# Whole levels of the sigmoid: from VectorE and ScalarE by turns to GpSimd alone, in a two-layer cross-attention and feed-forward kernel

## What is computed

```python
def act_qdq(x):
    scale = jnp.maximum(jnp.max(jnp.abs(x)) / qmax, 1e-12)
    return jnp.clip(jnp.round(x / scale), -qmax - 1.0, qmax) * scale
def fixed_qdq_u16(x):
    scale = 1.0 / 65536.0
    return jnp.clip(jnp.round(x / scale), 0.0, 65535.0) * scale
x = act_qdq(x)
up = act_qdq(x @ lpbq_dequant(w_up).T)
gate = act_qdq(x @ lpbq_dequant(w_gate).T)
sig = fixed_qdq_u16(jax.nn.sigmoid(gate))
gate = act_qdq(gate * sig)
o = act_qdq(gate * up)
return o @ lpbq_dequant(w_down).T
```

## Time and profile before

| | us |
|---|---|
| median of three runs (lowest, highest) | 1559.03 (1558.42, 1559.81) |
| the profiled execution's own time | 1561.33 |
| its span in the profile | 1559.6 |
| busy in the span: PE, DVE, ACT, POOL | 1280.5, 1042.2, 809.1, 522.7 |

### The profile page before, as it was taken

The page is one execution under the profiler, slowest core; times in us unless marked ns, Lnnn a source line. Parts: engine busy times, 40 slices in busy tenths (PEclk is TensorE's granted clock), DMA queues, the critical chain, the costliest instruction groups (busy, mean ns, idle before and its releaser), DMA issues. The chain is left out here.

```text
span 1559.6 us, 29136 instructions
## 1 busy us (share of the span) xinstructions
PE 1280.5 (82%) x8823; PEld 967.2 (62%) x8824; DVE 1042.2 (67%) x1908; ACT 809.1 (52%) x1173; POOL 522.7 (34%) x430
## 2 busy tenths in 40 slices
PE   5859899967987574989699999552399999999996
PEld 3426667753433364856366766552399989899895
DVE  4947997765589695548488888555156566656653
ACT  0535455654499596525477777551144343444431
POOL 1026677600000000010476766077223323333233
PEclk9979999988999556968899999655699999999998
DMA  5010000000033674000122122545222222222220
GB/s 207 1 65 1 1 0 0 0 1 0 0 122 161 212 237 164 9 1 0 58 69 83 65 70 92 217 167 186 84 46 49 45 47 44 45 42 51 47 42 9
DMA packets 63213, 106.87 MB, mean 69 GB/s; under 512 B 9712, under 2 KB 50768, under 8 KB 62000
## 3 DMA queue, kind: packets, MB, share of 16 engines
q1 hardware_dynamic: 48848, 89.17, 17.2%
q0 software_dynamic: 14304, 16.93, 6.1%
HBM read 67.89 MB, written 40.01 MB: 69 GB/s over the span
## 5 line engine op out<-in xcount | busy, mean ns | idle before, releaser
L2125 POOL DMA_INDIRECT out<-ex_yo,ex_mt x78 | 132.1, 1693 | 320.0 <-DVE ex_yo L2100 172.8
L2002 PE MATMUL ex_ps_h<-ex_xT_hi,a_arena 128*128 128x256 f16 x1248 | 212.8, 274 | 0.0
L2044 ACT ACTIVATE ex_hT<-ex_ps_h,e_b1T,e_unscale 128x256 f32<-128x256 f32 x312 | 150.9, 564 | 115.4 <-PE ex_ps_h L2002 115.4
L708 PE MATMUL at_ps_s<-a_arena,at_xnT_hi 128*128 (+1 forms) x512 | 162.8, 401 | 34.0 <-issue 26.7
L730 PE MATMUL at_ps_y<-c_VW,at_pT_hi 128*128 (+1 forms) x1024 | 171.1, 273 | 1.3 <-DVE main_x_res L857 1.3
L2002 PE MATMUL ex_ps_h<-ex_xT_lo,a_arena 128*128 128x256 f16 x624 | 171.1, 274 | 0.0
L2015 PE MATMUL ex_ps_y<-a_arena,ex_hT_lo 128*128 x624 | 170.1, 273 | 0.0
L2015 PE MATMUL ex_ps_y<-e_w_lo,ex_hT_hi 128*128 x624 | 170.1, 273 | 0.0
L2015 PE MATMUL ex_ps_y<-a_arena,ex_hT_hi 128*128 x624 | 170.1, 273 | 0.0
L976 POOL TENSOR_TENSOR at_sc<-at_sc,at_ri 128x960 f32<-128x960 f32 (+1 forms) x96 | 133.4, 1403 | 83.5 <-DVE at_ri L852 83.2
L1217 PE MATMUL gm_bank<-f_xq,f_wide 128*128 (+1 forms) x576 | 129.1, 384 | 20.8 <-ACT gm_stg L1255 16.2
(11 more groups left out here) (321 smaller groups left out, 2847.8 us busy)
## 6 DMA issues: line engine op xcount, KB each, us to landing
at_half<-in_L_ffn_W SPq DMA_DIRECT2D x32, 512.0 KB, 4.3
up_scratch<-gm_stg SPq DMA_DIRECT2D x16, 768.0 KB, 3.2
gm_stg<-up_scratch SPq DMA_DIRECT2D x16, 768.0 KB, 4.3
ex_row<-xs SPq DMA_DIRECT2D x39, 260.0 KB, 2.7
rt_stage<-in_L_ffn_W SPq DMA_DIRECT2D x16, 512.0 KB, 5.3
main_x_res<-in_x SPq DMA_DIRECT2D x8, 512.0 KB, 11.9
out<-main_x_res SPq DMA_DIRECT2D x4, 1024.0 KB, 12.3
xs<-rt_pad SPq DMA_DIRECT2D x18, 130.0 KB, 2.3
```

What stands on the lines that cost most here:

```text
L708: last = nc.tensor.matmul(ps_s[j][:, c * CH:(c + 1) * CH], a[:, d, :], b[:, d, bass.ds(off + c * CH, CH)], start=(n == 0), stop=(n == 3 * ...
L2002: last = nc.tensor.matmul(ps_h[:, n, :], a[:, bass.ds(e * WN + d * HID + n * P, P)], b[:, d, :], start=(m == 0), stop=(m == 3 * DT - 1))
L2044: last = nc.scalar.activation(hT[:, n, :], ps_h[:, n, :], ACT.Relu, bias=b1T[:, bass.ds(e * HT + n, 1)], scale=unscale[:, 0, bass.ds(e, 1)])
L2125: nc.gpsimd.indirect_dma_start(out=acc[:, :], out_offset=bass.IndirectOffsetOnAxis(ap=mt[j][:, q, 1:2].bitcast(U32), axis=0), in_=yo[j][:, ...
```

## The change

POOL makes the levels of all sixteen units; the halves of DVE and ACT and the semaphore `sqa_r` are gone. Product(u) waits for POOL's count.

```diff
@@ block.scalar
-                def sig_levels(u):
-                    act.wait_ge(sig_r, u + 1)
-                    nc.scalar.activation(sq[u % 2][:, :], unit(u), ACT.Copy, scale=65536.0).then_inc(sqa_r, 1)
@@
                 for u in range(NU):
                     up_out(u)
                     sigmoid(u)
-                    if u % 2:
-                        sig_levels(u)
                     if u + 1 < NU:
                         levels(u + 1)
@@ block.vector
-                def sig_levels(u):
-                    dve.wait_ge(sig_r, u + 1)
-                    nc.vector.tensor_scalar(sq[u % 2][:, :], unit(u), 65536.0, 65535.0, ALU.mult, ALU.min).then_inc(sq_r, 1)
                 def product(u):
-                    dve.wait_ge((sq_r, sqa_r)[u % 2], u // 2 + 1)
+                    dve.wait_ge(sq_r, u + 1)
                     nc.vector.tensor_tensor(unit(u), gq[u % 2][:, :], sq[u % 2][:, :], ALU.mult).then_inc(pr_r, 1)
@@
                 for u in range(NU):
                     up_max(u)
-                    if u % 2 == 0:
-                        sig_levels(u)
                     if u:
                         prod_max(u - 1)
                     product(u)
@@ block.gpsimd
                 for i in range(2):
                     nc.gpsimd.tensor_copy(ctxe[0:C1, i, :], ctxT[0:C1, 1, :]).then_inc(low_set, 1)
+                for u in range(NU):
+                    pool.wait_ge(sig_r, u + 1)
+                    need(pool, pr_r, u - 1)
+                    nc.gpsimd.tensor_scalar(sq[u % 2][:, :], unit(u), 65536.0, 65535.0, ALU.mult, ALU.min).then_inc(sq_r, 1)
                 pool.wait_ge(gred, 2)
                 nc.gpsimd.partition_all_reduce(allr[:, 1:3], red[:, 1:3], P, RMAX).then_inc(gall, 1)
```

More of the change, by code:

```diff
@@ L1201, in gated_mlp @@
             u_st = [z.sem(f"u_st{h}") for h in range(2)]
-            sqa_r = z.sem("sqa_r")
             gq_r, sig_r, sq_r, pr_r = z.sem("gq_r"), z.sem("sig_r"), z.sem("sq_r"), z.sem("pr_r")
```

## The result

| | before | after |
|---|---|---|
| median of four runs, us | 1559.34 (1558.42 to 1559.81) | 1588.29 (1587.93 to 1601.68) |
| span of the profiled execution | 1559.6 | 1599.9 |
| first to last all-reduce of scope "gu" | 93.63 | 124.82 |

The kernel is slower by 28.95 us: the ratio is 1.0207, with a 95% interval of 1.0154 to 1.0261, so the slowdown is clear and whether it is over 2% is not. That is outside the predicted range and on the side of the slow rival.

The account below looks back on a forecast made before the run. DVE was taken to bound the stretch: 7.16 us gained in the run, 6.71 lost before product(0) and 2.65 at the end gave +2.2, so 1559.0 + 2.2 = 1561.2 us, range 1554.7 to 1564.6.

Parts of the forecast that it names:

- the slow rival: POOL's level instruction exceeds 3.2 us and sets the beat with the product; at X = 4.0 1577.1 us, 18 slower; chance 0.12.
- What bounds the stretch: From 433 to 523 us DVE bounds the stretch, busy 85.85 of 90 us; product to product takes 4.99.
- relief for ACT: Removing ACT's eight copies gains nothing: its 4.66 us a unit stay hidden under DVE's 4.99.
- the sum: 7.16 us gained in the product steps, 6.71 lost before product(0), 2.65 at the end: +2.2 us.
- X = 2.3: Price in us of each of POOL's sixteen level instructions, taken from POOL's copy of 256 columns scaled to 1536.
- X up to 3.2 is hidden: DVE's two maxima hide a POOL level instruction up to 3.2 us, keeping the beat 4.99; 2.3 leaves 0.9 to spare.
- The rival's price for a unit: When POOL's level instruction exceeds 3.2 us, a unit takes X + 1.76 instead of 4.99; chance 0.12.
- They take turns whole: POOL's instruction and DVE's two-input product wait for each other at SBUF, so POOL starts unit u+2 when product(u+1) ends.
- The two loads: POOL library loads before the first level instruction, 8.5 us, and before the last all-reduce, 7.5 us.
- traffic and price go together: POOL's library loads cost more beside DMA traffic: 5.89 us in the quiet case, 7.58 to 9.86 in the other three.
- POOL first at the start: POOL's second level instruction precedes product(0), which starts at 445.6 instead of 438.89; with traffic-laden loads, chance 0.42.
- what follows product(15): Last level ends at 519.5, a 7.5 us load follows; the all-reduce starts at 527.0 against 524.82, 2.2 us later.

Follow-up runs that it names:

- e5: Changed kernel with POOL's level instruction as a plain copy, without scaling and clamp: stretch between all-reduces 86.96 us, kernel 1552.24 us against 1558.12 before.
- e2: Kernel before plus seven forms of POOL's instruction in the first stretch, at 1536 and 768 columns: at 1536 the change's form took 5.42 us, copies 1.46.
- e7: Changed kernel with POOL's level instruction as a two-input addition of 128, taken off in the product, no clamp: stretch 94.44 us, products 4.99 apart.
- e8: Kernel before with POOL making units 2 to 13 by the addition of 128, no clamp: 1554.30 us against 1558.12, ratio 0.9974.
- e6: Changed kernel with one arithmetic step in POOL's level instruction, clamp left out: stretch 106.37 us, products 5.74 apart.
- e3: Changed kernel with product(u) replaced by a maximum over `sq`, a single SBUF input: stretch 107.05 us, level instructions 5.37 to 5.42.
- e1: Changed kernel run again unedited on another chip: 1607.18 us against 1574.96 for the kernel before, ratio 1.0215.
- e4: Kernel before plus one single-column tensor_scalar on POOL behind the last product: stretch 97.53 us against 93.63.

## Why the prediction was wrong

**What bounds the stretch: right.** DVE did, and relief for ACT is worth nothing. Taking the level instruction off DVE at no other price gained 6.67 us (e5) where the sum had 7.16 less 0.5.

**X = 2.3: the step that failed.** "The nearest is POOL's copy", I wrote, and took its time, with the two-input operation as the bound above, 2.85. Measured: 5.42 (after, e2), over twice that, and so far over the 3.2 that DVE hides that POOL and its turns with the product set the beat. No row of the trace before was of this form, and I took for granted that an instruction with one input is cheaper than one with two. Here it is not: 1.46 for the copy, 2.75 for two inputs (e7, e8), 4.09 and 5.42 for one input with one and two arithmetic steps (e2). My 2.85 for two inputs from 1024 columns was near; my 2.35 for the copy from 256 was not.

**X up to 3.2 is hidden, beyond it POOL sets the beat: right as far as it was tried.** At X = 2.75 it was 4.99 (e7), at 4.09 it was 5.74 (e6), at 5.42 it was 7.02; nothing between 2.75 and 4.09 was run. The rival's price for a unit, X + 1.76, was 0.11 to 0.16 too high; X + 1.6 to 1.65 fits. The 1.61 us from POOL's end to DVE's in the earlier trace rows had been the nearer number.

**They take turns whole: right for this loop, too strong as a rule.** 5.42 becomes 6.95 beside a two-input product and stays 5.37 beside a one-input reduction (e3). SBUF — State Buffer of the Trainium skill (the section on the two sides) has the rule, an exclusive lock of the port pair held for a whole instruction, against a VectorE operation with two SBUF inputs; by that rule, the traces agree that one of the two waits, and not always that it waits to the end: where POOL was first, DVE's product had its turn before POOL's one-step form had ended (e2, e6), and the one at 397.66 in e2 ran inside POOL's instruction.

**The two loads: right in kind, mis-sized.** The first is 6.82 us, not 8.5, the second 5.94, not 7.5. I had read "traffic and price go together" out of four rows. In the runs since, the elementwise library took 6.8 to 7.1 us ahead of the level instruction with a DMA share of 0.33 or 0.34 beside it, no more than the 6.9 of e2 with 0.00. The all-reduce's took 5.8 to 6.2 with any share from 0.00 to 0.45, and 6.55 with 0.71 (e7). But the library alone does not decide either. The same traces have the loads of the earlier trace rows again: ahead of line 144 7.2 to 8.1 us, ahead of the second attention's addition of line 989 9.4 to 10.7 wherever "issue" ended it, ahead of the router's all-reduce (line 1698 before) 7.4 to 8.0 with a share of 0.80 to 0.84. So a high share goes with a longer load of the all-reduce's library, one like that of this stretch does not, and what makes line 989's so long stays open. GPSIMD Engine Reference of the Trainium skill (section 2.1) has about 6 us; for the all-reduce's library at low shares that agrees, for the elementwise one in this stretch it is 0.8 to 1.1 us short, and for those of lines 144, 989 and 1698 1.2 us or more.

**POOL first at the start: wrong in this kernel.** Product(0) was issued 0.05 us before POOL's second instruction and went first, in both profiled executions (0.04 in e1); in e6 and e7 POOL's second was issued 0.04 and 0.01 us before the product and went first. So the one issued first had its turn first in all four; what makes POOL's second instruction late with two arithmetic steps (0.08 us behind the first, where e6 has none) was not tried.

Put into the same steps, the missing number gives nearly the whole result. With X = 5.42 my own formulas, on the axis of before, have product(0) at 441.0 + 2 x 5.42 = 451.84, fifteen steps of 7.18 to 559.54, and the all-reduce 7.5 later at 567.04: +42.2. Measured was +31.2. The 11.0 between them are POOL first (5.4), the beat of 7.02 (2.3), the first load (1.7) and what follows product(15), 5.91 instead of 7.5 (1.6).

The slow rival, "POOL's instruction is longer than the 3.2 us it may take", is what happened. It had 0.12, and its size was set at X = 4.0 and +18. The words for it, "two arithmetic steps", named a part of the cause: the second step is 1.33 of the 5.42, and with one step alone the 4.09 is over 3.2 as well. Its "converts to 16 bits" was no part of it (5.42 against 5.38). The argument against it, "even the two-input operation scales to 2.85", was the failed step once more.

## What to carry to other kernels

When work moves to an engine on which the trace shows no instruction of the same form, the price of another form is no bound: widen the range by a factor rather than by a microsecond, and ask from which price on the new engine sets the beat. Count what an elementwise instruction on GpSimd brings beside itself: a library load before it and one before the next all-reduce, which are free only where POOL is idle long enough on both sides (e4, e8), and a turn at the port beside every two-input VectorE operation, and beside a one-input tensor_scalar as in e2. Keep the first and last units of such a loop on their old engines, and choose the form by its measured time (e7, e8).

## What the runs showed of the hardware that I had not expected

- On GpSimd, at 128 x 1536 and with nothing of VectorE in the way: tensor_scalar with two steps 5.42 us, with one step 4.09, a two-input addition with a constant per partition 2.75, a copy 1.46. Conversion to 16 bits changed none of these forms by more than 0.04 us (e2).
- The time has a fixed part of about 0.2 us (an estimate from the 768 and 1536 columns of e2), so that scaling from a small instruction overstates it: 2.35 us from 256 columns for a copy that took 1.46.
- A copy and a memset need no load; tensor_scalar and tensor_tensor do, and the next all-reduce then needs one again. In this stretch a load cost 5.8 to 7.1 us from the end of POOL's last instruction, however small the instruction that caused it (0.19 us in e4).
- VectorE's one-input tensor_scalar waited for GpSimd too (3.09 us instead of 0.75, e2), its maxima did not (1.74 to 1.76 in every run).
- An instruction that waits at the port is shown as a longer instruction and not as idle time: 6.95 for POOL's in the changed kernel, 4.77 for DVE's in e6.
